# A two-layer graph kernel on one core: the last residual add moves from VectorE into TensorE's accumulation

## The reference, cut to what matters

```python
# 50000 nodes x 128 floats, 12500 edges sorted by dst, 8 relation types
x1 = layernorm(x + L0(x, edge_attr, src, dst))        # mean of messages per dst, over the degree
h = x1
for l in range(2):                                     # relational attention, layers 0 and 1
    out_j = (h @ W[l, type])[src]                      # one of 8 matrices per edge
    logit = leaky_relu(q_part[dst] + k_part[src], 0.2)
    alpha = segment_softmax(logit, dst)
    h = relu(segment_sum(alpha * out_j, dst) + bias[l])
return layernorm(x1 + h)
```

## Time and profile before

| | us |
|---|---|
| median of 3 runs | 1012.64 |
| lowest, highest | 1012.32, 1015.95 |
| the profiled execution, whole | 1007.88 |
| its span, first to last instruction | 1006.1 |
| its mean granted TensorE clock | 0.84 |

### The profile page before, as it was taken

How to read it: one execution, slowest core, us unless ns; L and a number is a source line. 1 busy time by engine, 2 the same in 40 slices (tenths; PEclk the granted TensorE clock), 3 DMA queues, 4 the chain that set the end, 5 groups by cost and what they waited for, 6 DMA issues and landing times.

```text
span 1006.1 us, 10944 instructions
## 1 busy us (share of the span) xinstructions
PE 699.3 (70%) x2896; PEld 442.9 (44%) x2896; DVE 815.6 (81%) x2176; ACT 613.3 (61%) x1396; POOL 577.4 (57%) x506
## 2 busy tenths in 40 slices
PE   3546566657553798988977878289799867667840
PEld 3435455445443454555644545255455433333320
DVE  3589999988998869789889995868878878789850
ACT  1659999879998465555856675556446553434421
POOL 4767777777721788787000000387878606768773
PEclk9658777777875799999989999589999987789875
DMA  7276766765542232236325445322232411142210
GB/s 217 82 225 193 218 188 200 207 205 165 178 152 91 89 98 65 86 101 208 112 90 161 139 140 162 90 93 66 67 96 83 160 40 37 52 123 67 84 36 23
DMA packets 87742, 122.99 MB, mean 122 GB/s; under 512 B 14175, under 2 KB 66827, under 8 KB 87680
## 3 DMA queue, kind: packets, MB, share of 16 engines
q1 hardware_dynamic: 69455, 99.35, 31.4%
q0 software_dynamic: 15680, 21.55, 7.8%
q10 hardware_dynamic: 2544, 1.38, 0.6%
HBM read 87.79 MB, written 45.04 MB: 132 GB/s over the span
## 4 chain that ended last, share of the span: by engine, by line
DVE 34%; ACT 16%; PE 14%; POOL 14%; issue 12%; DMA 9%; SPq 1%; POOLq 0%; DVEq 0%; ACTq 0%
POOL xs L456 11%; ACT stage L786 8%; PE ps_y L705 7%; DVE ys L1108 6%; DVE work L1282 4%; DVE st L1057 3%; DVE st L1089 3%; ACT xd L802 3%; DVE ys L1255 3%; DMA stage<-in_x 2%; DVE stage L1051 2%; ACT ys L751 2%; POOL xd L456 2%; DVE opT L1282 2%; DMA out<-stage 2%
## 5 line engine op out<-in xcount | busy, mean ns | idle before, releaser
L786 ACT ACTIVATE stage<-stage,nm,rs 128x128 f32<-128x128 f32 x800 | 319.5, 483 | 11.5 <-DVE nm L1042 10.8
L705 PE MATMUL ps_y<-work,wr 128*128 128x512 f32 (+1 forms) x528 | 241.9, 590 | 59.6 <-DVE work L1282 59.3
L456 POOL DMA_INDIRECT xs<-h_table,posI x98 | 126.5, 1290 | 196.3 <-DMA h_table<-ys 166.8
L705 PEld LDWEIGHTS ps_y<-work,wr 128*128 128x128 f32 x528 | 101.0, 206 | 170.1 <-DVE work L1282 85.6
L456 POOL DMA_INDIRECT xs<-x_table,posI x98 | 125.9, 1284 | 65.1 <-DMA x_table<-xd 35.5
L523 POOL DMA_INDIRECT out<-xd,outI x98 | 117.8, 1202 | 78.6 <-DMA out<-stage 36.1
L1282 DVE SCALAR_TENSOR_TENSOR work<-typB,xs 128x896 f32<-128x896 uint8 x132 | 142.7, 1085 | 15.2 <-PE ps_y L705 7.1
L705 PE MATMUL ps_y<-opT,wr 128*128 128x512 f32 (+1 forms) x256 | 118.8, 590 | 22.7 <-DVE opT L1282 22.7
L456 POOL DMA_INDIRECT xs<-in_x,srcI x98 | 101.1, 1031 | 47.5 <-issue 27.7
L456 POOL DMA_INDIRECT xd<-in_x,dstG x98 | 104.4, 1065 | 30.1 <-issue 28.6
L1047 DVE BATCH_NORM_STATS2 st<-stage 128x6 f32<-128x128 f32 x400 | 82.9, 278 | 30.4 <-DMA stage<-in_x 30.1
(11 more groups left out here) (206 smaller groups left out, 1161.3 us busy)
## 6 DMA issues: line engine op xcount, KB each, us to landing
stage<-in_x SPq DMA_DIRECT2D x39, 640.0 KB, 4.2
out<-stage SPq DMA_DIRECT2D x39, 640.0 KB, 3.1
xs<-alpha_rows SPq DMA_DIRECT2D x28, 448.0 KB, 4.8
x_table<-xd SPq DMA_DIRECT2D x14, 448.0 KB, 3.1
h_table<-ys SPq DMA_DIRECT2D x14, 448.0 KB, 4.4
work<-in_src SPq DMA_DIRECT2D x13, 448.0 KB
ys<-in_edge_attr SPq DMA_DIRECT2D x6, 896.0 KB, 8.6
sameB<-same_rows SPq DMA_DIRECT2D x42, 112.0 KB, 3.3
```

What stands on the lines that cost most here:

```text
L456: nc.gpsimd.indirect_dma_start(out=buf[:, t, :], out_offset=None, in_=table, in_offset=bass.IndirectOffsetOnAxis(ap=idx[:, t:t + 1], axis= ...
L705: mm = pe.matmul(ps_y[:, u, lo:hi], wr[:, r, :], rows, start=(r == 0), stop=(r == R - 1))
L786: ins = a.activation(slot(c)[:, r, :], slot(c)[:, r, :], ACT.Identity, bias=nm[:, h, n:n + 1], scale=rs[:, h, n:n + 1])
```

## The change: what it does

The addition of x1[dst] in the second layer goes from DVE to PE. `back_rows` computes each tile of `ps_t` as ys turned (a product with the identity) plus a second product, identity times the `xd` tile, accumulated in the same place. DVE takes its statistics from `ps_t`, ACT normalizes from `ps_t` into `xd`. So `ps_t` is given free by `f_rows[2]`, after ACT's seven normalizations, and no longer by `last_used`, after DVE's addition.

```diff
@@ back_rows (PE)
                     if j == 0:
                         ps_t_free((f_rows[1], g + 1), (f_qs[1], g + 1))
                     else:
-                        ps_t_free((last_used, g + 1))
+                        ps_t_free((f_rows[2], g + 1))
                     for t in range(G):
-                        mm = pe.transpose(ps_t[:, t * P:(t + 1) * P], ys[:, g * G + t, :], ident)
+                        o = ps_t[:, t * P:(t + 1) * P]
+                        if j:
+                            pe.matmul(o, ys[:, g * G + t, :], ident, start=True, stop=False)
+                            mm = pe.matmul(o, ident, xd[:, g * G + t, :], start=False, stop=True)
+                        else:
+                            mm = pe.transpose(o, ys[:, g * G + t, :], ident)
@@ last_norm (ACT)
                     act.wait_ge(f_rs, g + 1)
-                    norm_rows(xd, g, g % 2, XD, f_rows[2])
+                    for t in range(G):
+                        ins = a.activation(xd[:, g * G + t, :], ps_t[:, t * P:(t + 1) * P], ACT.Identity,
+                                           bias=nm[:, g % 2, XD + t:XD + t + 1], scale=rs[:, g % 2, XD + t:XD + t + 1])
+                    ins.then_inc(f_rows[2], 1)
@@ last_rows (DVE)
                     dve.wait_ge(g_T[1], g + 1)
-                    T.step(TT(cols_of(xd, g), ps_t[:, 0:GD], cols_of(xd, g), ALU.add))
-                    dve.sem_inc(last_used, 1)
-                    row_stats(xd, g, g % 2, XD)
+                    for t in range(G):
+                        T.of(v.bn_stats(st[:, g % 2, XD + t, :], ps_t[:, t * P:(t + 1) * P]))
                     sums(g, XD, XD + G).then_inc(f_sum, 1)
```

More of the change, by code:

```diff
@@ L260, in graph_layers @@
         g_scan = [sem(f"g_scan{j}") for j in range(2)]; g_act = [sem(f"g_act{j}") for j in range(2)]
-        g_T = [sem(f"g_T{j}") for j in range(2)]; last_used = sem("last_used")
+        g_T = [sem(f"g_T{j}") for j in range(2)]
         refill = sem("refill")
```

## The result

| | us |
|---|---|
| before, median of 4 runs (range) | 1014.3 (1012.32 to 1016.9) |
| changed, median of 4 runs (range) | 1026.11 (1024.46 to 1027.22) |
| ratio, 95% interval | 1.0114, 1.0083 to 1.0145 |
| the same pair later, 10 and 19 runs | 1023.25 and 1015.41 |
| ratio, 95% interval | 1.0066, 1.0031 to 1.0100 |

The first four runs fall 1.1 us above the range. The longer series puts the loss at 6.7 us by its ratio and at 7.8 us between its medians, and its 1023.25 us lies inside the range. Ratios leave out executions in the chip's slower state; in the sets whose times are read, that is one of 12 of xd_tr_third (1426.41 us).

A forecast was written before the change was run, and what follows sets the result against it. It took DVE and PE both to lie on the last part's path, decided group by group. Terms +6.0 + 3.8 − 0.9 − 1.9 − 1.1 − 1.5 = +4.4 us on 1012.64 gave 1017.0, range 1006 to 1025.

The forecast's parts named there:

- What bounds the stretch, and who is last where: Last part, from about 797 us: DVE and PE both on the path, each arriving last at 7 of 14 groups.
- DVE's 17.2 us and PE's added 2.3 us a group: Removed addition frees DVE 1.23 us in each of 14 groups; PE's group grows from 0.93 to 3.2 us at full clock.
- The ring with ACT: Groups 8 to 10: PE waits for ACT's normalization, 9.3 us per group against 9.95, gain 0.6 each, −1.9 for three.
- The clock: PE idles less, so one slow pair of products keeps full clock, −1.5 us; groups 1 and 13 start cold, +1.9 each.
- Statistics from PSUM: DVE's statistics read from ps_t were costed at nothing more; 0.4 us a group stayed in the range.
- rival 2: Statistics from PSUM cost 0.4 us more in all 14 groups: +10.3 us, 1023; chance 0.20.
- Hidden weight loads: PE's weight loads of 190 ns overlap, so each added instruction costs 110 ns.
- rival 3: Weight loads not hidden beside 128 columns: 5.4 us a group, +33 in all, 1046; chance 0.04.
- Rival 1: Intended gain: added PE pass is cheap, 1.7 us a group, DVE last nearly everywhere: −10.5 us, 1002; chance 0.12.
- rival 4: Warmer PE: three or more slow pairs keep the full clock, 0 or less in sum, 1012; chance 0.14.
- Slot 51: turn_rows of group 13 waits some 1.5 us more for ACT, costed at nothing because ACT takes its result later.
- The level: The +4.4 us was added to a median of 1012.64 us for the kernel before, giving 1017.0.

The follow-up runs named there:

- xd_tr_third: Changed kernel with wide xd products ahead of the relu wait and sums turned by adding transposes, third timing; ratio 0.9964 to the kernel before.
- pe_only: PE's 28 instructions a group as in the changed kernel, DVE still making one pass into xd for its statistics; ratio 1.0205 to the kernel before.

## Why the prediction was wrong, point by point

- **What bounds the stretch, and who is last where: right.** DVE's wait for PE came to 41.5 us in 12 groups, forecast about 40 in 12 or 13. Group 4 alone kept the whole saving, −1.5.
- **DVE's 17.2 us and PE's added 2.3 us a group: right.** The first product of each pair in the changed kernel, and its statistics (ns, min/median/max):

```profile
L670 PE MATMUL ps_t<-identS,ys x196: 272/275/580, 808.3 to 998.0; 128*128 128x128 f32 x196
...
L1270 DVE BATCH_NORM_STATS2 st<-ps_t x98: 277/280/300, 811.6 to 999.8; 128x6 f32<-128x128 f32 x98
```

  Two instructions follow two every 0.223 us at the full clock (940.35 to 940.58), 112 ns each and not 110. At the full clock a group took 3.3 us (3.29 without a wait ahead of it, 3.36 behind one) and not 3.2. That is some 1.5 us over the groups where PE is last.
- **The ring with ACT: the mechanism right, the term mis-sized.** It gave 0.3 a group and not 0.6: 6.13 us from statistics to the end of ACT (forecast 6.0), 0.14 until PE starts, 3.36 for PE. That is +1.0 us on the sum for three groups, half of it the longer group of the point above. The prediction put group 11 with those where PE alone is last; the ring sets it too. Its +1.0 came out right (+1.0), but by luck: the ring's 9.62 us stands in place of 8.66 + 1.0.
- **The clock: the step that failed.** I took one slow pair as regained, −1.5, and counted groups 1 and 13 at 4.85 us. Group 1 started at the full clock (+0.6 in place of +1.9) and group 3 ran behind faster products (+0.2 in place of +1.0). But group 2 fell into a slow stretch, and in group 13 PE stayed at half for longer than in the stretch the price came from. The table by stretch of the changed kernel: the stretch and its length, busy us (instructions) of PE, PEld, DVE, ACT and POOL, then the granted clock, here 0.50; first in group 13, then in group 2:

```profile
992.80:997.40 4.60, 4.54 (x21) 4.54 (x22) 0.00 (x0) 0.01 (x1) 3.67 (x4) 0.50 0.15 50
...
845.40:847.30 1.90, 1.90 (x10) 1.81 (x9) 0.29 (x1) 0.64 (x1) 0.00 (x0) 0.50 0.09 22
```

  Group 13 started at 992.86 and took 5.7 us, in the second profile 6.3. What groups 1 and 3 gave (−2.1 against the forecast), groups 2 and 13 took back (+1.6), and the slow products ahead of groups 5 and 7 cost up to 1.4 more there: the eight ahead of group 7 took 4.68 us in one profile of the changed kernel and 6.10 in the other. On balance the clock gave nothing of the 1.5 and took some 0.8 more (from the unrounded intervals). The price of group 1 was right and the place was not: in pe_only that group did start at half and took 4.99 us, forecast 4.85, but in the second profile of the kernel before its seven transposes took 0.96 us, at a granted clock of 1.00, behind the same idle 2.85 us as in the earlier trace rows. So which groups run slowly changes between executions of one kernel, and one profile could not tell it.
- **Statistics from PSUM: right, rival 2 falls.** Seven take 1.49 us against 1.45, 0.04 a group where that rival had 0.4. The 62 cycles between the two sources of the Trainium skill, "VectorE: DVE Perf Modes", section on the TRN2 errata, would be 6.3 us in 98 statistics, as an estimate from it; the traces show some 0.5 us. The 1023 us of rival 2 stand beside a measured 1023.25, which is chance: its mechanism is not there.
- **Hidden weight loads: right, rival 3 falls.** Instructions follow at 112 ns although a load lasts about 190. Rival 1 falls with pe_only, and rival 4 with the balance of the clock.
- **Slot 51: nearly right.** `turn_rows` of group 13 waited 1.2 us for ACT and no later step shows it.
- **The level: missed.** The forecast +4.4 was put on 1012.64, a median of three; the kernel before has 1015.4 over 19 runs. On that level 1019.8 would have stood against 1023.25. And the range did not allow for the scatter of single executions; nor does it quite hold what it says it holds, since rival 2 with both groups at half clock is 1022.9 + 2.8 = 1025.7.

So the direction was right, a loss rather than the gain that DVE's share suggests, and its size, +4.4, was a little over half of the 7.9 of the end stretch. Of the missing 3.5 us, 1.5 are the clock's credit, which did not come; 0.8 are the balance of the six groups that the clock moved (1, 2, 3, 5, 7 and 13); 1.3 are the ring in groups 8 to 11, with group 11's normalization counted there; the rest cancels. PE's slightly longer group is contained in these. That split is worked out from intervals; no run isolates the clock. The steps that failed are thus the clock's −1.5, with the places it was counted in, and the ring's 0.6 a group.

The time itself, 1026.11, lies 9.1 us above 1017.0. Beside the 3.5 us, 1.7 are the level of the kernel before in that set (1014.3 and not 1012.64), and 3.9 are what the two medians of four differ by outside the end stretch (11.8 and not 7.9), which the longer series does not show. More than half of that miss is therefore scatter between executions and not the mechanism.

## What to carry to other kernels

Moving work from the busiest engine to a less busy one pays only where the first is last; count, group by group, who comes last, and price the added work in instructions of the receiver. A place that one profile shows as slow may be fast in the next execution, so a gain that hangs on the clock needs more than one profile. If a step has an operand that is ready early, do that part ahead of the wait, and check what else shares the slot before moving a step forward in an in-order queue. Look at who becomes last once the path is shorter: here it was the queue of scatters, which no forecast had counted. Compare short stretches of traces where whole times scatter by as much as the effect.

## What the runs showed of the hardware that was not expected

- A float32 transpose accumulates onto products in PSUM (start=False), with one instruction a tile: seven in 0.93 us. The same as products costs fourteen instructions, 1.72 us. With the xd products ahead of the wait, that turned a loss of 0.7% into a gain of 0.4%, and into one of 1.2% with the five moved slots.
- 14 instructions of 128 columns and 4 of 512 and 384 take nearly the same time for 896 columns: the groups are 0.1 us apart.
- ACT's normalization of a tile takes 463 ns from PSUM where it took 478 from SBUF, and seven in a row 2.56 us against 2.81.
